# A twelve-stage decoder kernel: each stage's normalisation moves into the end of the stage before it, and so do its first loads

## The reference, cut to what matters

```python
def _layernorm(x, axis=-1, eps=1e-05):
    m = jnp.mean(x, axis=axis, keepdims=True)
    v = jnp.var(x, axis=axis, keepdims=True)
    return (x - m) / jnp.sqrt(v + eps)

x = x + _L0_attn_ref(_layernorm(x), ...)          # stage 0
x = x + _L0_xattn_ref(_layernorm(x), ctx_512, ...) # stage 1
x = x + _L0_ffn_ref(_layernorm(x), ...)           # stage 2
...                                               # L1, L2, L3: 3 stages each
```

## Time and profile before

| | |
|---|---|
| median of 3 runs | 3798.62 us |
| profiled execution | 3795.66 us |
| its span in the trace | 3793.9 us |
| PE busy, share of the span | 88% |
| DVE | 46% |
| ACT | 35% |
| POOL | 11% |
| DMA, mean over the span | 39 GB/s |

### The profile page before, as it was taken

One profiled execution on the slowest core, in us unless ns is written; L12 is line 12 of the kernel. 1 busy time (PEld: TensorE's weight loads), 2 busy tenths in 40 slices (PEclk: granted clock), 3 DMA queues, 4 the chain that ended last, 5 costly groups with the idle time before them and its releaser, 6 DMA issues. The chain is left out here.

```text
span 3793.9 us, 57228 instructions
## 1 busy us (share of the span) xinstructions
PE 3341.5 (88%) x22669; PEld 2153.3 (57%) x22673; DVE 1759.0 (46%) x3531; ACT 1318.5 (35%) x2217; POOL 419.5 (11%) x278
## 2 busy tenths in 40 slices
PE   5479999995999879999999789989999997458799
PEld 3256777775455444577777457754677776134444
DVE  2624555553222245566664333345566663544322
ACT  0114566550111132466664112222566662113221
POOL 0211222210000034200000000014100000103000
PEclk6669999997999989999999899999999998578899
DMA  1022222210111112111110110021111111000111
GB/s 26 1 72 58 60 59 60 58 36 25 34 42 42 29 31 63 28 49 48 48 48 19 47 40 26 26 67 28 40 49 48 48 48 36 0 16 8 40 38 37
DMA packets 182683, 149.42 MB, mean 39 GB/s; under 512 B 77445, under 2 KB 155127, under 8 KB 181122
## 3 DMA queue, kind: packets, MB, share of 16 engines
q1 hardware_dynamic: 182418, 145.77, 14.0%
HBM read 110.32 MB, written 13.37 MB: 33 GB/s over the span
## 5 line engine op out<-in xcount | busy, mean ns | idle before, releaser
L1371 ACT ACTIVATE l2x_shared<-l2x_shared,l2x_a_low 128x1500 f32<-128x1500 f32 x112 | 173.1, 1545 | 189.4 <-DVE l2x_shared L1327 189.4
L1371 ACT ACTIVATE l1x_shared<-l1x_shared,l1x_a_low 128x1500 f32<-128x1500 f32 x112 | 173.1, 1546 | 188.4 <-DVE l1x_shared L1327 186.2
L1371 ACT ACTIVATE l0x_shared<-l0x_shared,l0x_a_low 128x1500 f32<-128x1500 f32 x112 | 173.3, 1547 | 187.5 <-DVE l0x_shared L1327 180.7
L1262 PE MATMUL l0x_a_T_ps<-ident,l0x_shared 128*125 128x128 f32 x1344 | 176.1, 281 | 15.5 <-issue 14.7
L1262 PEld LDWEIGHTS l0x_a_T_ps<-ident,l0x_shared 128*125 128x125 f32 x1344 | 155.2, 187 | 39.6 <-issue 38.0
L1262 PE MATMUL l2x_a_T_ps<-ident,l2x_shared 128*125 128x128 f32 x1344 | 176.5, 281 | 0.8 <-ACT l2x_shared L1371 0.8
L1262 PE MATMUL l1x_a_T_ps<-ident,l1x_shared 128*125 128x128 f32 x1344 | 176.5, 281 | 0.8 <-ACT l1x_shared L1371 0.8
L1246 PE MATMUL l2x_a_S_ps<-l2x_kt,l2x_a_q 64*128 64x375 f32 x896 | 172.1, 501 | 1.2 <-DVE l2x_shared L1327 0.7
L1246 PE MATMUL l1x_a_S_ps<-l1x_kt,l1x_a_q 64*128 64x375 f32 x896 | 172.2, 501 | 0.5 <-DVE l1x_shared L1327 0.5
L1246 PE MATMUL l0x_a_S_ps<-l0x_kt,l0x_a_q 64*128 64x375 f32 x896 | 172.1, 501 | 0.5 <-DVE l0x_shared L1327 0.5
L1262 PEld LDWEIGHTS l1x_a_T_ps<-ident,l1x_shared 128*125 128x125 f32 x1344 | 155.2, 187 | 29.8 <-issue 28.2
(11 more groups left out here) (672 smaller groups left out, 6100.8 us busy)
## 6 DMA issues: line engine op xcount, KB each, us to landing
l0f_gu<-in_L_ffn_gu SPq DMA_DIRECT2D x36, 256.0 KB, 2.6
l0x_a_q<-l0x_qa SPq DMA_DIRECT2D x64, 96.0 KB, 2.7
l1x_a_q<-l1x_qa SPq DMA_DIRECT2D x64, 96.0 KB, 2.2
l2a_w<-in_L_attn_qkv SPq DMA_DIRECT2D x16, 384.0 KB, 3.0
l2x_a_q<-l2x_qa SPq DMA_DIRECT2D x64, 96.0 KB, 2.2
l0x_raw<-in_ctx SPq DMA_DIRECT2D x16, 375.0 KB
kv_rotated<-l0x_v SPq DMA_DIRECT2D x16, 375.0 KB
kt_rotated<-l0x_kt SPq DMA_DIRECT2D x16, 375.0 KB, 4.9
```

The source lines that it names most:

```text
L1262: last = pe.transpose(T_ps[0:KP, g, kk * 128:(kk + 1) * 128], p[:, n % 2, j % HJ // 3 * 2 + j // HJ, j % 3 * KP:(j % 3 + 1) * KP], m.ident[:])
L1371: act.activation(p[:, n % 2], p[:, n % 2], ACT.Exp, bias=low[:, n % 2, 1:2], scale=-1.0, accum_out=den[:, b % 2, k:k + 1]).then_inc(exp_re ...
```

## The change

- A stage function becomes a generator. It first allocates its tiles and yields a `Head`: a name, the list of first loads, and whether transposes are wanted. Its own call of `layernorm` is gone.
- `Line.run` drives the twelve generators. The ending of stage k calls `follow()`, which runs stage k+1 up to its `Head`, with tiles allocated from the other side of on-chip memory, so that both stages' tiles live side by side.
- `Ending` is the normalisation in pieces, for pairs of tiles. In the block that ends a stage SP issues the next stage's loads and waits for them, DVE runs `moments(g)` behind the addition of pair g and `norms(g - 1)` behind that, ACT runs the roots and the copies to `m.ht`, PE the transposes. Its nine semaphores belong to the ending's scope. The first stage still calls `layernorm`.
- The table for the square root is loaded early in the ending's ACT stream.
- The weight slots of the query parts are now a view of a tile `space`, which later holds `attend`'s `pt`; their four semaphores move to `latent_cross`'s outer scope, which had none.
- `w_o` and `w_v` are no longer asked for at the start of the query block but behind refill i = 5 of 8 (stage 1) or n = 8 of 16 (stages 4 and 7).

```diff
+class Ending:
+    def fetch(self, sp):
+        for dst, source in self.head.loads:
+            sp.dma_start(dst, source).then_inc(self.loaded, 16)
+    def arrive(self, sp):
+        if self.head.loads:
+            sp.wait_ge(self.loaded, 16 * len(self.head.loads))
+    def moments(self, dve, g, added, count):
+        m, mv = self.m, self.m.moments
+        dve.wait_ge(added, count)
+        for t in (2 * g, 2 * g + 1):
+            dve.bn_stats(self.stats[:, t, :], m.x[:, t, :]).then_inc(self.stats_done, 1)
+        for t in (2 * g, 2 * g + 1):
+            dve.wait_ge(self.stats_done, t + 1)
+            dve.bn_aggr(mv[:, t, :], self.stats[:, t, :]).then_inc(self.moments_done, 1)
+        dve.wait_ge(self.moments_done, 2 * g + 2)
+        dve.tensor_scalar(self.std[:, 2 * g:2 * g + 2], mv[:, 2 * g:2 * g + 2, 1], 1e-5, None,
+                          ALU.add).then_inc(self.var_ready, 1)
+    def norms(self, dve, g):
+        m, mv = self.m, self.m.moments
+        dve.wait_ge(self.std_ready, g + 1)
+        dve.reciprocal(self.rstd[:, 2 * g:2 * g + 2], self.std[:, 2 * g:2 * g + 2]).then_inc(self.rstd_ready, 1)
+        dve.wait_ge(self.rstd_ready, g + 1)
+        for t in (2 * g, 2 * g + 1):
+            dve.tensor_scalar(m.xn[:, t, :], m.x[:, t, :], mv[:, t, 0:1], self.rstd[:, t:t + 1],
+                              ALU.subtract, ALU.mult).then_inc(self.normed, 1)
+    def turns(self, pe, g):
...
+        pe.wait_ge(self.normed, 2 * g + 2)
...
+        for c in range(DC):
+            for k in range(2):
+                last = pe.transpose(ps[:, c * 256 + k * 128:c * 256 + (k + 1) * 128],
+                                    self.m.xn[:, 2 * g + k, c * 128:(c + 1) * 128], self.m.ident[:])
+        last.then_inc(self.turned, 1)
+    def copies(self, act, g):
...
+        act.copy(self.m.ht[:, :, g * 256:(g + 1) * 256],
+                 self.tp[g % len(self.tp)][:].rearrange("p (c n) -> p c n", c=DC)).then_inc(self.copied, 1)
@@ project_add
             @block.tensor
             def _(pe):
                 for g in range(4):
...
                     last.then_inc(product, 1)
+                    if g > 1:
+                        ending.turns(pe, g - 2)
+                ending.turns(pe, 2)
+                ending.turns(pe, 3)
@@ project_add
                     dve.tensor_tensor(m.x[:, 2 * g:2 * g + 2, :], m.x[:, 2 * g:2 * g + 2, :], ps[g][:],
                                       ALU.add).then_inc(added, 1)
+                    ending.moments(dve, g, added, g + 1)
+                    if g > 0:
+                        ending.norms(dve, g - 1)
+                ending.norms(dve, 3)
@@ plain_queries
                     for dst, source in arrivals(i):
                         sp.dma_start(dst, source).then_inc(loaded[i % 4], 16)
+                    if i == 5:
+                        ahead.fetch_outputs(sp)
@@ roped_queries
+                    if n == 8:
+                        ahead.fetch_outputs(sp)
@@ l2_ffn
                     dve.scalar_tensor_tensor(m.x[:, t, :], o_ps[:, 0:D], os[:], m.x[:, t, :],
                                              ALU.mult, ALU.add).then_inc(added, 1)
+                    if t % 2:
+                        ending.moments(dve, t // 2, added, t + 1)
+                for g in range(4):
+                    ending.norms(dve, g)
```

More of the change, by code:

```diff
@@ L148, in _, with __init__, follow, run @@
                             last.then_inc(turned, 1)
+class Head:
+    def __init__(self, name, loads, turn=True):
+        self.name, self.loads, self.turn = name, loads, turn
+class Line:
+    SIDES = ("left", "right")
+    def __init__(self, nc, stages):
+        self.nc, self.stages = nc, stages
+        self.now, self.head = 0, None
+    def follow(self):
+        if self.now + 1 < len(self.stages):
+            self.nc.default_side = self.SIDES[(self.now + 1) % 2]
+            self.head = next(self.stages[self.now + 1])
+            self.nc.default_side = self.SIDES[self.now % 2]
+        return self.head
+    def run(self, m):
+        for k, stage in enumerate(self.stages):
+            self.now = k
+            self.nc.default_side = self.SIDES[k % 2]
+            if self.head is None:
+                head = next(stage)
+                layernorm(self.nc, m, head.name, m.x, head.turn, head.loads)
+            self.head = None
+            for _ in stage:
+                pass
+        self.nc.default_side = self.SIDES[0]
@@ L394, in project_add, with _ @@
         with nc.Block() as block:
+            @block.sync
+            def _(sp):
+                ending.fetch(sp)
+                ending.arrive(sp)
             @block.tensor
@@ L1460, in gated_ffn @@
         squashed += [squashed[-1] + product_first]
+    head = m.line.follow()
     with Stage(nc) as st:
@@ L1470, in gated_ffn @@
         out = [[st.ps(f"{name}out{c}{g}", [128, 512]) for g in range(2)] for c in range(DC)]
+        ending = head and Ending(st, m, head, [out[c][g] for c in range(DC) for g in range(2)])
+        added = st.sem(name + "added")
         arrived = [st.sem(f"{name}arrived{j}") for j in range(3)]
@@ L1543, in _ @@
                     last.then_inc(turned, 1)
+                if ending:
+                    for g in range(4):
+                        ending.turns(pe, g)
             @block.scalar
@@ L2007, in l2_attention @@
         out = [[st.ps(f"l2a_out{c}{g}", [128, 512]) for g in range(2)] for c in range(DC)]
+        ending = Ending(st, m, m.line.follow(), [out[c][g] for c in range(DC) for g in range(2)])
+        added = st.sem("l2a_added")
         o_arrived = st.sem("l2a_o_arrived")
@@ L2361, in l2_ffn @@
         o_ps = st.ps("l2f_o_ps", [128, 512])
+        ending = Ending(st, m, m.line.follow(), [st.ps(f"l2f_lt_ps{k}", [128, 512]) for k in range(2)])
         done = st.sem("l2f_h_done")
```

211 lines of the change are left out of this document (154 added, 57 removed).

## The result

The changed kernel takes 3737.9 us (median of four runs, 3734.1 to 3742.0), the kernel before 3795.5 us beside it (3791.1 to 3800.0): a ratio of 0.985, interval 0.983 to 0.987. The profiled executions have spans of 3793.9 and 3736.1 us, so 57.8 us are to be found in the traces. Medians are of the runs at the usual clock: one run of the kernel before (3874.5 us, mean granted clock 0.88) and one of `l2f_gap` (5417.4 us, 0.59) are left out.

A forecast was written before the change was run, and what follows sets the result against it. PE, busy for 88% of the span, bounds the kernel; the change works in the other 12%. Savings of 28.8 + 15.5 + 15.3 + 0.9 = 60.5 us give 3735, predicted as a 3738 us median, range 3717 to 3759.

The forecast's parts named there:

- The sum: Whole kernel: all terms together save 60.5 us, from the profiled execution's 3795.66 us to 3735, plus 3.0 for the median.
- Slow projections: Borders out of stages 0, 1, 4, 7: all but the last pair's normalisation is hidden, loads come early; 28.8 us saved.
- (d): Rival: loads are not early, so idle times at four blocks return, 14 us; 3752 us, chance 0.03.
- Fast additions: Ends of stages 3, 9, 10: DVE becomes the bound at 2.85 us a pair; 12.3 us saved.
- a loss of 0.5: Ends of stages 2, 5 and 6: cutting the dense pass into pairs eats the saved meeting; -0.5 us for all three.
- Stage 8: Stage 8's end: after the last addition come moments, four norms, transposes, copy and meeting; 3.7 us saved.
- The moved weights: Query parts of stages 1, 4, 7: slot waits of 11.48 and twice 1.9 us go, 15.3 us; fewer clears 0.9.
- need 8 to 12 us: Stage 1's query block: 1.5 MB plus the 0.6 MB slot load in this time at 174 to 277 GB/s, before PE's 17.4 us.
- (a): Rival: in stage 1 the refill behind the outputs is late instead; up to 11.5 us come back, 3750 us, chance 0.09.
- The clock: PE's clock at block starts: bounded by 20 us gained or 9 us lost, taken as zero.
- (b): Rival: PE's clock holds through the tail, seven blocks start at 2.4 GHz, 2.9 us each; 3718 us, chance 0.10.
- (c): Rival: the sparse tail drops PE's clock and the next stage doesn't regain it; slower, 3825 us, chance 0.02.

The follow-up runs named there:

- l2f_gap: Changed kernel with stage 8's moments of pairs 0 to 2 in VectorE's wait for the next product and all four roots ahead of ScalarE's copies: 3731.3 us.
- dense_ends: Changed kernel with endings kept in the same block but normalising all eight tiles in one pass after the additions, except in stage 8: 3750.4 us.
- loads_only: Changed kernel with early loads kept in each stage's last block, but the old eight-tile normalisation run as a block of its own: 3769.3 us.
- late_outputs: Changed kernel with the latent stages' output weights asked for at the query block's start again, ahead of the fourth weight slot: 3753.2 us.
- the short filler: Changed kernel with two or three added PE products ahead of the last two pairs' transposes at projections, one behind the last transposes: 3732.2 us.
- busy_tail: Changed kernel with three to six added PE products in the tails of projections into stages 1, 2, 4, 5 and 11, one behind the last transposes: 3739.3 us.
- four_slots: Changed kernel with all four weight slots of the query parts asked for in the tail of the stage before, instead of three: 3733.8 us.
- combined: Changed kernel with the fourth slot asked for early, stage 8's moments and roots moved, and dense passes at ends of stages 2, 5, 6: 3725.8 us.

## Why the prediction was right, point by point

**The sum.** 60.5 us were predicted and 57.8 came. Their misses, in the order of the table, are +1.4, +1.0, -4.6, +2.2, -1.2 and -1.5: the small sum of misses is in part luck. That 3738 meets 3737.9 is luck besides: I added 3.0 us because the median of three runs lay that far above the profiled execution. With the fourth run the median before is 3795.5, where the profiled execution lies, and the changed kernel's two figures agree as well. The 3.0 us that weren't there made up for the 2.7 us that didn't come.

**Slow projections** (28.8, measured 30.2). Out of stage 4 the tail from last addition to next product was to be 6.85 us (7.65 less the 0.8 of delay) and is 6.1: VectorE's part takes 2.9 us where I had 3.2, since the third pair's tiles run while ScalarE takes the fourth's root; transposes and copy take 1.3 for 1.55, the meeting 1.85 for 2.1. The first pair's transposes delay the last product by 0.44 us, not 0.8 (the last pitch is 7.35 us where the others are 6.91). That would make 10.2 us; the part got only 8.9 shorter, because the first addition comes 10.1 us behind the first product where it was 8.8. The clock's record explains it: 5.9 us of that stretch run at 0.50, where it was 3.3. dense_ends confirms that these ends live from the pairs, loads_only that the loads were hidden behind them. No load came late, so (d) is out.

**Fast additions** (12.3 for stages 3, 9 and 10, measured 13.3). The additions in stage 3's projection:

```profile
1371.05 0.69 DVE L545 TENSOR_TENSOR x<-x,l1a_o_out 128x512 f32<-128x512 f32 x1 [4.71 <-PE l1a_o_out L526]
...
1373.53 0.69 DVE L545 TENSOR_TENSOR x<-x,l1a_o_out 128x512 f32<-128x512 f32 x1 [0.58 <-PE l1a_o_out L526]
...
1376.18 0.68 DVE L545 TENSOR_TENSOR x<-x,l1a_o_out 128x512 f32<-128x512 f32 x1
...
1378.82 0.68 DVE L545 TENSOR_TENSOR x<-x,l1a_o_out 128x512 f32<-128x512 f32 x1
...
1385.37 3.32 PE L1060 MATMUL l1x_q_plain_ps<-ht,l1x_space 128*128 128x448 f32 x4 [1.95 <-PEq L66]
```

VectorE is the bound as said: 2.64 us for a pair where I had 2.85, and 14.3 us from the first addition to the next product, as predicted. At the ends of stages 2, 5 and 6 the smaller pitch turns a loss of 0.5 into a gain of 1.7. (The 0.5 was not worked out: by my own 0.4 for stage 2, three such ends were 1.2.) That the pairs eat the meeting there was the right mechanism; without them the gain would be some 5 us.

**Stage 8** (3.7, measured -0.9). This step failed. I wrote of its end only "the last addition ends at 3353.19, then 1.2 + 4 x 1.0", and said nothing of the moments of pairs 0 to 2. They are inserted between an addition and the next tile's first step, on the engine that is on the chain of this loop: 3 x 1.23 = 3.7 us. The earlier trace rows shows VectorE waiting 6.98 us before each addition; I had the room in front of me and did not ask on which side of it the new work stood. The other 0.9 us is a root queued behind a copy on ScalarE, an order of the change that I had not read. l2f_gap gives both back.

**The moved weights** (15.3 and 0.9, measured 15.0). The mechanism is right (late_outputs). The step that slot and context "need 8 to 12 us" was too kind. The slot landed 18.5 us after the first product (273.25 less 254.71), and PE was there after 16.5, not 17.4: a wait of 2.06 us in stage 1 stayed. 2.1 MB in 18.5 us are 114 GB/s, under the 174 that I had taken for the slow end. Yet the windows of the changed kernel from 254.7 to 273.3 us have 3.4 MB moved, 183 GB/s, within my range. The 1.3 MB more can only be of loads that SP asked for behind the slot, from 263.56 us on: they took part of the rate before the slot had landed whole. My sum had given them nothing. Behind the slot PE waits for no load, so (a) is out. The Trainium skill, "DMA: Bandwidth & Descriptors" (queues, rings and completion order), has each engine take descriptors in ring order; the 13.59 us of late_outputs against 2.06 agree.

**The clock** (0, measured -1.5 in the parts that no edit touches, and part of the rest). By the clock's record all eleven blocks start at 0.50. Before, ten did; stage 3 started at the full clock, behind sixteen transposes in a row, and has lost it. The windows at stage 3's start, first in the kernel before, then in the changed one:

```profile
1309.00:1313.00 4.00, 3.08 (x8) 1.01 (x8) 0.00 (x0) 0.58 (x1) 0.00 (x0) 1.00 0.01 2
```

```profile
1285.00:1289.00 4.00, 3.13 (x4) 0.98 (x5) 0.00 (x0) 0.00 (x0) 0.00 (x0) 0.50 0.00 0
```

Its first part is 1.2 us longer. So (b) is out. In stages 3 to 7, 9 and 10 the clock is up again 3 to 6 us behind the first product; in stages 1, 2 and 11 it stays down for 15, 44 and 22 us, where it was 17, 44 and 22. So (c) is out. What the profile could not tell me, it tells now: gaps of 2.4 us in the tail and 2.5 us at the meeting, with 1.3 us of transposes between them, bring the half clock on; with the first gap filled the second does not. The Trainium skill, "TensorE: Matmul & The Clock Gate" (HAM oscillation), says that waits between bursts make each burst start cold; the trace agrees at stages 4 and 5 in both directions (0.50 behind the gaps, 1.00 with the first one filled). At stage 11 the evidence is weaker: with the short filler it starts at the full clock and falls a microsecond later, and its router takes 16.6 us against 17.5, but 16.7 in dense_ends without any filler. Nor is a filler the only way: dense_ends starts stage 4 at the full clock too, behind sixteen transposes in a row, and its query part takes 142.8 us. Filling the gap is worth 1 to 3 us at a border here, but only where the filler ends before the data come.

**What stays open.** Parts that no edit touches differ by up to 4 us from one profiled execution to the next: stage 3's core takes 58.1, 59.7 or 61.0 us, stage 3's first part 23.9 to 27.9, stage 10's core 60.3 or 62.3. In the windows the clock's rise comes earlier or later. What decides it was not tried. A difference of under 2 us between two kernels in the length of a part is therefore worth something only where rows of the edited place bear it out.

## What to carry to other kernels

Before normalising pair by pair behind an addition, look at what ends the idle time between two additions: where a product does, the pairs are free and only the last one counts; where nothing does, a dense pass is shorter, and only the saved meeting is gained. New work in a loop goes behind the engine's longest wait, not behind the step whose result it needs. And on a queue, ask for what is needed first, first: the output weights cost 15 us in three stages by standing, 2.5 MB, ahead of a slot that was needed sooner.

## What the hardware showed that I had not expected

PE can stay at half the clock while it is busy without a gap. In busy_tail stage 1 starts at the full clock and loses it at 255.6 us, among small products (64 columns):

```profile
252.00:256.00 4.00, 2.58 (x22) 2.41 (x23) 0.84 (x2) 0.00 (x0) 0.00 (x0) 0.95 0.17 46
256.00:260.00 4.00, 4.00 (x21) 3.77 (x21) 0.42 (x1) 0.27 (x1) 0.00 (x0) 0.50 0.54 170
```

The second row has no idle time at 0.50. What made the clock fall is not shown: the first row still holds two short waits (1.32 and 0.51 us, the last of them 1.3 us before the fall). This query part gained nothing from the filler (62.8 and 62.0 us against 61.6), and the 10 us that I had named as possible there did not come. It gets the clock back at another time in each execution, mostly between 270 and 281 us: in four_slots at 275.3, 24.6 us behind its first product, in combined at 270.7, 15.5 us behind its own. That is most of the 4.4 us between their query parts.

The count in a grouped row is of instructions, and a float32 product here is two of them (a transpose is one): the row x12 above is six products, 5.32 us at the full clock. I had sized the filler by the "x8" in 3.27 us of the earlier trace rows, read as eight products.
